# A decoder layer in one kernel: the cross-attention readout as three rounded products, standing between two groups of transposes

## The chip, the cores and the metric

The kernel runs on one core of a Trainium2 chip. The metric is the device time of one execution in microseconds (us). The core's engines work side by side, each through its own queue in order: PE (TensorE) multiplies matrices, and PEld is its loading of the stationary operand; DVE (VectorE) and ACT (ScalarE) do element work; POOL (GpSimd) does element work and issues indirect transfers; SP (SyncE) issues plain transfers. They wait for each other through semaphores, and a waiting instruction holds all that stands behind it on its engine.

## The reference

A pre-norm decoder layer for 32 batches of 128 tokens with 512 features, in float32. Three residual steps follow each other:

```
x = x + attention(layernorm(x))        # differential attention with rotary q and k
x = x + readout(layernorm(x), ctx)     # cross-attention on 128 context rows per batch
x = x + experts(layernorm(x))          # 48 experts, top 8 of each token
```

The step that the change touches is the second:

```
scores  = einsum('bsd,bmd->bsm', hidden, memory) * scale     # masked
attn    = softmax(scores)
readout = einsum('bsm,bmd->bsd', attn, memory)
```

`memory` is `ctx_2048`, one matrix of 128 rows by 512 per batch. The readout is one product of a 128x128 matrix of probabilities with that matrix.

## The kernel before

The first stage runs over the 32 batches in 38 turns. In each turn six batches stand at six different places of the layer: `norm` (batch t), `project` (t-1), `attend` (t-2), `cross` (t-3), `route` (t-4) and `slots` (t-5). The code calls them n, p, a, c, r and s. The first eight and the last turns are written out, the ones between are a hardware loop over pairs of turns. The second stage runs over the 48 experts and follows when all tokens are scattered into `slot_records`.

The order on each engine is written by hand: the function `turn` of each engine lists its instructions, and nothing reorders them. `x.after(b, "name")` in a wait is the semaphore count at which step `name` of batch b is done.

PE ends a turn with the transposes of q and of k (`transpose4`, L1170, into the PSUM banks `bank_tb` and `bank_ta`), then the readout (L1316). The next turn begins with the transposes of the normalized x, also into `bank_ta`; these wait until ACT has copied k out of that bank (`prj_a`, step `kT`). So the order around the bank is: probabilities transposed into `bank_ta` (L1300), copied by ACT to `xprobs_t`; k transposed into it, copied by ACT to `k_t`; x transposed into it. Then come the attention scores, which need `q_t` and `k_t`.

The readout is one float32 product of `xprobs_t` with `ctx_sb`; its records are two per batch. It writes `bank_r`, in which the router's counts stand too; it therefore waits until DVE has read these (`rte_v`, step `taken`, L1066). The projections are made otherwise (`product_r`, L1185): each operand is split into a high part, rounded to the type fp32r by an ACT copy, and a low part, the rest, made by a subtraction on DVE; three products high x high, high x low and low x high are summed in PSUM.

On DVE the end of a turn is: rotary sums (L1057, L1059), the counts `pos` and `taken` (L1064, L1066), `sq_mean` (L1070), a wait for POOL's `rstd_h` (L606), and `heads` (L1076), which PE transposes after the scores of the next turn.

On POOL a turn has eight indirect transfers (L544) and between them three powers for norms (L555: `rstd3` of the routed batch, `rstd1` of the new one, `rstd2` of the cross batch), a rotary sum (L598) and `rstd_h`. The transfer of row 0 waits for DVE's `token` (L850); `rstd2` is needed by DVE's `xn2` (L989), which PE transposes in the middle of the turn.

SP loads the context of the next cross batch in each turn, into one of two buffers; it waits until the readout of two batches ago is done.

## Time and profile before

| what | value |
|---|---|
| three runs | 1108.96, 1112.71 (median), 1113.69 us |
| profiled execution, first to last instruction | 1110.6 us |
| PE busy | 1032.1 us, 93% |
| DVE busy | 872.8 us, 79% |
| ACT busy | 628.9 us, 57% |
| POOL busy | 551.0 us, 50% |
| mean granted clock of PE | 0.981 |

The page gives the span of the profiled execution and no other time of it, so the span stands for its own time; the median of the runs is 2.1 us above it. Busy shares are means over both stages. The readout belongs to the first stage, which ends a little before 700 us. A row of a timeline gives start, length, engine, line of the kernel, output and input, and in brackets how long the engine had been idle before it and what ended that. Lengths of PE instructions overlap, since they are pipelined; the distance of two starts is what one costs in a row of them.

### The profile page before, as it was taken

How to read it: one execution, taken by the hardware profiler on the slowest of the kernel's cores; microseconds unless marked ns; L12 is line 12 of the kernel's file. 1: busy time of each engine (PE TensorE's matmuls, PEld its weight loads, DVE VectorE, ACT ScalarE, POOL GpSimd, SP SyncE). 2: the span in 40 equal slices, each digit the busy share in tenths (PEclk: the TensorE clock that was granted, in tenths of full speed). 3: DMA queues.
4: the chain of work that ended last, by engine and by line, in shares of the span. 5: the costliest groups of instructions: out<-in, count | busy, mean ns of one | idle time of the engine just before them, and what ended most of it. 6: DMA issues, size and time to landing. Idle time of an engine off the chain costs nothing.

```text
span 1110.6 us, 24896 instructions
## 1 busy us (share of the span) xinstructions
PE 1032.1 (93%) x6564; PEld 835.1 (75%) x6564; DVE 872.8 (79%) x2430; ACT 628.9 (57%) x1751; POOL 551.0 (50%) x529
## 2 busy tenths in 40 slices
PE   5999899999999999999999977999999999999892
PEld 4777777878878788787887856887777778778781
DVE  5777798888888798888888864677877778787771
ACT  4555445555554554555545441576767767676661
POOL 2124566666666666666666666333433334343333
PEclk9999899999999999999999998999999999999996
DMA  7999574543313122121221210599999999999983
GB/s 287 356 299 288 178 270 161 206 152 138 115 54 96 47 70 72 47 95 47 76 66 49 77 39 20 184 257 246 255 244 246 245 246 256 240 260 241 238 179 46
DMA packets 94051, 185.71 MB, mean 167 GB/s; under 512 B 24791, under 2 KB 24791, under 8 KB 93504
## 3 DMA queue, kind: packets, MB, share of 16 engines
q1 hardware_dynamic: 62640, 145.10, 40.2%
q0 software_dynamic: 31376, 40.20, 17.2%
q8 instruction: 16, 0.26, 0.1%
q14 instruction: 19, 0.16, 0.0%
HBM read 116.00 MB, written 122.00 MB: 214 GB/s over the span
## 4 chain that ended last, share of the span: by engine, by line
PE 26%; DMA 26%; issue 18%; POOL 13%; DVE 10%; ACT 3%; POOLq 1%; DVEq 1%; SPq 0%; ACTq 0%
DMA layer_out<-qk_both,scatter_idx 21%; PE ps L1185 13%; POOL slot_records L544 6%; PE ps L1170 5%; POOL layer_out L625 4%; DVE qk_both L1001 3%; POOL rstd L555 3%; PE ps L1175 2%; PE ps L1316 2%; DMA x_ln<-in_x 2%; PE ps L1212 1%; DVE diff L996 1%; PE ps L1283 1%; DMA slot_records<-row,slot_idx 1%; DMA w_raw<-slot_records 1%
## 5 line engine op out<-in xcount | busy, mean ns | idle before, releaser
L544 POOL DMA_INDIRECT slot_records<-row,slot_idx x256 | 266.1, 1040 | 88.5 <-issue 59.6
L625 POOL DMA_INDIRECT layer_out<-qk_both,scatter_idx x96 | 143.3, 1493 | 256.2 <-DVE scatter_idx L1102 205.3
L555 POOL TENSOR_TENSOR rstd<-mv,neg_half 128x1 f32<-128x1 f32 x96 | 80.0, 833 | 130.2 <-DVE mv L914 78.7
L1185 PE MATMUL ps<-w_high,xn_high 128*128 128x512 f32 x384 | 114.9, 422 | 0.7 <-ACT xn_high L640 0.7
L675 ACT ACTIVATE probs<-ps,neg_max_s 128x128 f32<-128x128 f32 x256 | 90.1, 378 | 33.6 <-DVE neg_max_s L911 33.6
L1341 PE MATMUL ps<-w_high 128*128 128x192 f32 x576 | 90.6, 279 | 19.6 <-DVE w_low L1088 19.2
L1185 PE MATMUL ps<-w_low,xn_high 128*128 128x512 f32 x384 | 108.6, 405 | 0.0
L1185 PE MATMUL ps<-w_high,xn_low 128*128 128x512 f32 x384 | 106.9, 400 | 0.0
L1341 PEld LDWEIGHTS ps<-w_high 128*128 128x128 f32 x576 | 76.0, 191 | 40.0 <-issue 39.3
L640 ACT ACTIVATE xn_t<-ps 128x512 f32<-128x512 f32 x64 | 38.3, 599 | 117.7 <-PE ps L1170 117.7
L1088 DVE TENSOR_TENSOR w_low<-gu_sb,w_high 128x1536 fp32r<-128x1536 f32 x48 | 84.3, 1757 | 7.4 <-ACT w_high L640 4.9
L1341 PE MATMUL ps<-w_high,w_low 128*128 128x192 f32 x576 | 87.8, 274 | 0.0
L1341 PE MATMUL ps<-w_low,w_high 128*128 128x192 f32 x576 | 87.7, 274 | 0.0
L1375 PE MATMUL ps<-w_high 128*128 128x512 f32 x192 | 81.2, 423 | 2.8 <-DVE w_high L1088 2.8
L1185 PEld LDWEIGHTS ps<-w_low,xn_high 128*128 128x128 f32 x384 | 71.4, 192 | 14.6
L1185 PEld LDWEIGHTS ps<-w_high,xn_low 128*128 128x128 f32 x384 | 70.4, 190 | 13.9
L1375 PE MATMUL ps<-w_high,w_low 128*128 128x512 f32 x192 | 75.9, 395 | 0.0
L1341 PEld LDWEIGHTS ps<-w_low,w_high 128*128 128x128 f32 x576 | 75.9, 192 | 0.0
L1341 PEld LDWEIGHTS ps<-w_high,w_low 128*128 128x128 f32 x576 | 75.9, 192 | 0.0
L1001 DVE TENSOR_TENSOR qk_both<-ps,rope_tab 128x1024 f32<-128x1024 f32 x64 | 75.1, 1215 | 0.7 <-PE ps L1185 0.7
L1185 PEld LDWEIGHTS ps<-w_high,xn_high 128*128 128x128 f32 x384 | 66.9, 193 | 10.7 <-ACT xn_high L640 1.1
L640 ACT ACTIVATE w_high<-h 128x192 fp32r<-128x192 f32 x144 | 51.7, 363 | 40.0 <-DVE h L1110 37.7
(165 smaller groups left out, 2462.0 us busy)
## 6 DMA issues: line engine op xcount, KB each, us to landing
gu_sb<-in_gate_up SPq DMA_DIRECT2D x48, 768.0 KB, 5.5
slot_records<-dn_both SPq DMA_DIRECT2D x6, 3366.0 KB, 22.9
w_raw<-slot_records SPq DMA_DIRECT2D x48, 280.5 KB, 4.7
dn_both<-in_down_proj SPq DMA_DIRECT2D x48, 256.0 KB, 3.2
x_ln<-in_x SPq DMA_DIRECT2D x32, 256.0 KB, 2.8
x_res<-in_x SPq DMA_DIRECT2D x32, 256.0 KB, 3.1
ctx_t_sb<-in_ctx_t SPq DMA_DIRECT2D x32, 256.0 KB, 3.6
ctx_sb<-in_ctx_rows SPq DMA_DIRECT2D x32, 256.0 KB, 4.2
```

Of the source, the lines that this page charges most:

```text
L544: pool.indirect_dma_start(out=records, out_offset=bass.IndirectOffsetOnAxis(ap=slot_idx[:, s.parity, k:k + 1], axis=0), in_=row[:, s.parit ...
L555: pool.tensor_tensor(rstd[:, :], mv[:, 1:2], neg_half[:, 0:1], ALU.pow).then_inc(steps.sem, 1)
L625: pool.indirect_dma_start(out=out, out_offset=bass.IndirectOffsetOnAxis(ap=scatter_idx[0:PART[h], d.parity, h:h + 1], axis=0), in_=y[0:PAR ...
L640: act.activation(dst, src, ACT.Copy).then_inc(steps.sem, 1)
L675: last = act.activation(probs[:, s, h, :], blocks(banks_s[:, s, :])[:, h, :], ACT.Exp, bias=neg_max_s[:, s, h:h + 1], scale=INV_SCALING, a ...
L1001: dve.tensor_tensor(buf[:, :, :, :].rearrange("p g r f -> p (g r) f"), qk, rope_tab[:, i:i + 1, :].to_broadcast([P, 4 * NH2, NF]), ALU.mul ...
L1088: return dve.tensor_tensor(dst, src, high.bitcast(FP32), ALU.subtract)
L1170: last = pe.transpose(blocks(bank)[:, c, :], src(c), ident[:, :])
L1175: last = pe.matmul(dst, left(c), right(c), start=(c == 0), stop=(c == n - 1))
L1185: last = pe.matmul(dst, left[:, c, :], right[:, m, c, :], start=(n == 0 and c == 0), stop=(n == 2 and c == KC - 1))
L1341: last = pe.matmul(dst, left[:, u.parity, k, cols], right[:, u.parity, k, :], start=(n == 0 and k == 0), stop=(n == 2 and k == KC - 1))
L1375: last = pe.matmul(dst, left[0:n, d.parity, 0, part(h)], right[0:n, d.parity, 0, :], start=(i == 0), stop=(i == len(pairs) - 1))
```

## The change

The readout is computed as the projections are: from a high and a low part of the probabilities and a high and a low part of the context. ACT now copies the transposed probabilities to `xprobs_high` where it copied them to `xprobs_t`, and gets one more copy per turn, `ctx_high`, between `heads_high` and the exponentials of the scores. POOL gets one subtraction per turn, `ctx_low`, behind `rstd3`. DVE gets one subtraction per turn, `xprobs_low`, behind the rotary sums. PE makes three products in place of one, and they stand between the transposes of q and the transposes of k; these now wait for `xprobs_low`, since it reads `bank_ta`. SP's wait for the readout becomes two waits, for the scores and for `ctx_low`.

```diff
@@ sync: turn
                     if c.back(2).exists():
-                        sp.wait_ge(crs_t.sem, crs_t.after(c.back(2), "readout"))
+                        sp.wait_ge(crs_t.sem, crs_t.after(c.back(2), "scores"))
+                        sp.wait_ge(ctx_p.sem, ctx_p.after(c.back(2), "low"))
@@ gpsimd: turn
+                def context_low():
+                    if c.exists():
+                        pool.wait_ge(ctx_a.sem, ctx_a.after(c, "high"))
+                        if c.back(1).exists():
+                            pool.wait_ge(crs_t.sem, crs_t.after(c.back(1), "readout"))
+                        pool.tensor_tensor(ctx_low[:, :], ctx_sb[:, c.parity, :], ctx_high[:, :].bitcast(FP32),
+                                           ALU.subtract).then_inc(ctx_p.sem, 1)
...
                 scale(out_p, out_v, o, rstd3, mv3)
+                context_low()
                 if early:
                     scatter_ready()
@@ scalar: turn
                     copy(heads_high[:, :, :], heads_t[:, :, :], hds_a)
+                if c.exists():
+                    act.wait_ge(d_ctx[c.parity], moved(c, 2))
+                    if c.back(1).exists():
+                        act.wait_ge(crs_t.sem, crs_t.after(c.back(1), "readout"))
+                    copy(ctx_high[:, :], ctx_sb[:, c.parity, :], ctx_a)
...
                     act.wait_ge(crs_t.sem, crs_t.after(c, "probsT"))
-                    copy(xprobs_t[:, :], bank_ta[:, 0:P], crs_a)
+                    copy(xprobs_high[:, :], bank_ta[:, 0:P], crs_a)
@@ vector: turn
+                if c.exists():
+                    dve.wait_ge(crs_a.sem, crs_a.after(c, "probsT"))
+                    if c.back(1).exists():
+                        dve.wait_ge(crs_t.sem, crs_t.after(c.back(1), "readout"))
+                    dve.tensor_tensor(xprobs_low[:, :], bank_ta[:, 0:P], xprobs_high[:, :].bitcast(FP32),
+                                      ALU.subtract).then_inc(crs_l.sem, 1)
                 if r.exists():
 
                     dve.wait_ge(rte_t.sem, rte_t.after(r, "counts"))
@@ tensor: turn
                     transpose4(bank_tb, lambda k: rot[:, k * P:(k + 1) * P]).then_inc(prj_t.sem, 1)
+                if c.exists():
+                    pe.wait_ge(crs_a.sem, crs_a.after(c, "probsT"))
+                    pe.wait_ge(ctx_p.sem, ctx_p.after(c, "low"))
+                    if r.exists():
+                        pe.wait_ge(rte_v.sem, rte_v.after(r, "taken"))
+                    pe.matmul(bank_r, xprobs_high[:, :], ctx_high[:, :], start=True, stop=False)
+                    pe.matmul(bank_r, xprobs_high[:, :], ctx_low[:, :], start=False, stop=False)
+                    pe.wait_ge(crs_l.sem, crs_l.after(c, "low"))
+                    pe.matmul(bank_r, xprobs_low[:, :], ctx_high[:, :], start=False, stop=True)\
+                        .then_inc(crs_t.sem, 1)
+                if p.exists():
                     pe.wait_ge(rope.sem, rope.after(p, "imag_k"))
                     if c.exists():
-                        pe.wait_ge(crs_a.sem, crs_a.after(c, "probsT"))
+                        pe.wait_ge(crs_l.sem, crs_l.after(c, "low"))
                     transpose4(bank_ta, lambda k: rot[:, DM + k * P:DM + (k + 1) * P]).then_inc(prj_t.sem, 1)
-                if c.exists():
-                    pe.wait_ge(crs_a.sem, crs_a.after(c, "probsT"))
-                    if r.exists():
-                        pe.wait_ge(rte_v.sem, rte_v.after(r, "taken"))
-                    pe.matmul(bank_r, xprobs_t[:, :], ctx_sb[:, c.parity, :], start=True, stop=True)\
-                        .then_inc(crs_t.sem, 1)
```

PE, end of a turn and start of the next, before (the eight transposes of `qk_rot` are four of q and four of k):

```order
L1170 MATMUL ps<-ident,qk_rot 128x128 x8
L1316 MATMUL ps<-ctx_sb,xprobs_t 128x512
L1170 MATMUL ps<-ident,xn 128x128 x4
L1212 MATMUL ps<-k_t,q_t 128x128 x8
L1170 MATMUL ps<-ident,heads 128x128 x4
```

The same place of the changed kernel (its line numbers are some 28 higher):

```order
L1198 MATMUL ps<-ident,qk_rot 128x128 x4
L1341 MATMUL ps<-ctx_high,xprobs_high 128x512
L1342 MATMUL ps<-ctx_low,xprobs_high 128x512
L1344 MATMUL ps<-ctx_high,xprobs_low 128x512
L1198 MATMUL ps<-ident,qk_rot 128x128 x4
L1198 MATMUL ps<-ident,xn 128x128 x4
L1240 MATMUL ps<-k_t,q_t 128x128 x8
```

The readout has moved in front of the four transposes of k, and nothing stands any more between these and the transposes of x, which use the same bank.

DVE, end of a turn in the changed kernel:

```order
L1079 TENSOR_TENSOR qk_rot<-qk_both 128x16x32
L1081 TENSOR_TENSOR qk_rot<-qk_both 128x8x32
L1087 TENSOR_TENSOR xprobs_low<-ps,xprobs_high 128x128
L1092 TENSOR_TENSOR pos<-ps,taken 128x48
L1094 TENSOR_TENSOR taken<-ps,taken 128x48
L1098 TENSOR_SCALAR sq_mean<-sq_sum 128x4
L1104 TENSOR_TENSOR heads<-ps,rstd_h 128x512
```

Before, the same rows stood there without `xprobs_low`; `pos`, `taken`, `sq_mean` and `heads` are now behind it.

POOL, first half of a turn in the changed kernel:

```order
L562 TENSOR_TENSOR rstd<-mv,neg_half 128x1
L573 TENSOR_TENSOR ctx_low<-ctx_sb,ctx_high 128x512
L551 DMA slot_records<-row,slot_idx 9216x561
L562 TENSOR_TENSOR rstd<-mv,neg_half 128x1
L551 DMA slot_records<-row,slot_idx 9216x561
L562 TENSOR_TENSOR rstd<-mv,neg_half 128x1
L551 DMA slot_records<-row,slot_idx 9216x561 x2
```

Before, the same rows without `ctx_low`; two transfers and the powers `rstd1` and `rstd2` are now behind it.

## Rows read from the trace of the kernel before

**Rows 1.** Busy us by stage: span, PE, PEld, DVE, ACT, POOL, granted clock, DMA share, GB/s.
```profile
300.00:500.00 200.00, 197.72 (x1215) 157.56 (x1214) 174.35 (x562) 107.61 (x380) 127.22 (x131) 1.00 0.22 67
```

**Rows 2.** Timeline of PE: readouts of batch 3 and of batch 29; start, length.
```profile
127.42 1.02 PE L1316 MATMUL ps<-ctx_sb,xprobs_t 128*128 128x512 f32 x2
...
642.87 1.02 PE L1316 MATMUL ps<-ctx_sb,xprobs_t 128*128 128x512 f32 x2
```

**Rows 3.** Timeline of all engines, end of one steady turn, start of the next.
```profile
304.62 1.19 PE L1170 MATMUL ps<-ident,qk_rot 128*128 128x128 f32 x8
...
304.82 0.28 ACT L640 ACTIVATE xprobs_t<-ps 128x128 f32<-128x128 f32 x1
304.91 0.21 DVE L1066 TENSOR_TENSOR taken<-ps,taken 128x48 f32<-128x48 f32 x1
...
305.04 0.16 DVE L1070 TENSOR_SCALAR sq_mean<-sq_sum 128x4 f32<-128x4 f32 x1
305.15 0.42 PEld L1170 LDWEIGHTS ps<-ident,qk_rot 128*128 128x128 f32 x4 [0.17 <-ACT xprobs_t L640]
...
305.64 1.02 PE L1316 MATMUL ps<-ctx_sb,xprobs_t 128*128 128x512 f32 x2
305.95 0.62 ACT L640 ACTIVATE k_t<-ps 128x512 f32<-128x512 f32 x1
306.36 0.69 DVE L1076 TENSOR_TENSOR heads<-ps,rstd_h 128x512 f32<-128x512 f32 x1 [1.17 <-POOL rstd_h L606]
...
306.61 0.42 PEld L1170 LDWEIGHTS ps<-ident,xn 128*128 128x128 f32 x4 [0.78 <-ACT k_t L640]
306.62 0.66 PE L1170 MATMUL ps<-ident,xn 128*128 128x128 f32 x4
...
307.46 0.60 ACT L640 ACTIVATE xn_high<-ps 128x512 fp32r<-128x512 f32 x1 [0.68 <-PE ps L1170]
```

**Rows 4.** The same timeline: DVE and POOL element operations in the turn before.
```profile
301.57 0.28 DVE L1024 TENSOR_TENSOR xscore_kept<-ps,mask_sb 128x128 f32<-128x128 f32 x1
301.71 0.73 POOL L598 TENSOR_TENSOR qk_rot<-qk_both 128x256 f32<-128x256 f32 x1 [1.60 <-DVE qk_both L1001]
...
301.98 0.61 DVE L1032 TENSOR_TENSOR xscore<-xscore_kept,mask_bias 128x128 f32<-128x128 f32 x1
```

**Rows 5.** The same timeline: PE, lengths of rounded products and of four transposes.
```profile
308.29 0.66 PE L1170 MATMUL ps<-ident,heads 128*128 128x128 f32 x4
...
309.71 1.10 PE L1185 MATMUL ps<-w_low,xn_high 128*128 128x512 f32 x4
...
310.65 1.09 PE L1185 MATMUL ps<-w_high,heads_high 128*128 128x512 f32 x4
```

**Rows 6.** The same timeline, middle of the turn: ACT, POOL, DVE and PE.
```profile
309.79 0.63 ACT L640 ACTIVATE heads_high<-heads_t 128x512 fp32r<-128x512 f32 x1
...
311.43 0.37 ACT L675 ACTIVATE probs<-ps,neg_max_s 128x128 f32<-128x128 f32 x1 [1.01 <-DVE neg_max_s L911]
...
311.49 1.07 POOL L555 TENSOR_TENSOR rstd<-mv,neg_half 128x1 f32<-128x1 f32 x1 [2.66 <-DVE mv L914]
...
313.57 1.03 POOL L544 DMA_INDIRECT slot_records<-row,slot_idx  x1 [1.01 <-DVE row L850]
...
316.45 0.96 POOL L555 TENSOR_TENSOR rstd<-mv,neg_half 128x1 f32<-128x1 f32 x1
...
317.54 0.55 DVE L989 TENSOR_SCALAR xn<-x,mv,rstd 128x512 f32<-128x512 f32 x1 [0.42 <-POOL rstd L555]
...
318.27 0.49 PEld L1170 LDWEIGHTS ps<-ident,xn 128*128 128x128 f32 x4
```

**Rows 7.** Timeline of PE around 114 us.
```profile
113.89 1.12 PE L1170 MATMUL ps<-ident,row 128*128 128x128 f32 x4 [4.81 <-DVE row L931]
```

**Rows 8.** Busy time by stage, columns as in Rows 1.
```profile
110.00:120.00 10.00, 6.12 (x19) 5.03 (x20) 5.73 (x19) 1.41 (x2) 3.16 (x4) 0.66 0.55 198
```

**Rows 9.** Timeline around 41 us, before any readout existed.
```profile
41.11 0.63 PE L1170 MATMUL ps<-ident,xn 128*128 128x128 f32 x4 [0.99 <-ACT k_t L640]
```

More of the change, by code:

```diff
@@ L182, in decoder_layer @@
         xsum = sb("xsum", [P, 1])
-        xprobs_t = sb("xprobs_t", [M, P])
+        xprobs_high = sb("xprobs_high", [M, P], FP32R)
+        xprobs_low = sb("xprobs_low", [M, P], FP32R)
+        ctx_high = sb("ctx_high", [M, DM], FP32R)
+        ctx_low = sb("ctx_low", [M, DM], FP32R)
         xinv = sb("xinv", [P, 1])
@@ L302, in decoder_layer @@
         crs_a = Steps(sem("cross_scalar"), "xT exp probsT")
+        ctx_a = Steps(sem("context_scalar"), "high")
+        ctx_p = Steps(sem("context_pool"), "low")
+        crs_l = Steps(sem("cross_vector_low"), "low")
         out_v = Steps(sem("readout_vector"), "inv coef x2 stats aggr eps normed")
@@ L576, in turn @@
                 scale(out_p, out_v, o, rstd3, mv3)
+                context_low()
                 if early:
```

## The prediction, made before the changed kernel ran

> **What bounds the kernel now.** I read the busy time by stage first. From 300 to 500 us PE is busy 197.7 of 200 us, at the full granted clock, DVE 174.4, POOL 127.2 and ACT 107.6 [rows 1]. So in the first stage PE sets the pace, and the reader should see how little it idles: 2.3 us in about ten turns, 0.23 us a turn. The readouts of batch 3 and batch 29 start at 127.42 and 642.87 us [rows 2]: 26 turns in 515.5 us, 19.8 us each. All that makes PE wait longer in a turn is paid once per turn, if no later wait of PE takes it up.
>
> Then I read the timeline at the turn's end, where the change works [rows 3]. PE issues the eight transposes of q and k from 304.62, and those of k wait for ACT's copy of the probabilities, which ends at 304.82 + 0.28 = 305.10. The readout starts at 305.64. The next transposes (of x) start at 306.61, and what they waited for is not the readout but ACT's copy of k, which ends at 305.95 + 0.62 = 306.57. So the readout, 0.98 us from its start to the next one's, lies beside ACT's copies of q and k; PE would have been free only about 0.1 us earlier. The readout costs nearly nothing today, and it is the cover for the copy of k.
>
> **The change, part by part.** I work out when the transposes of x can start in the changed kernel, on the clock of the same turn.
>
> 1. The copy to `xprobs_high` stands where `xprobs_t` stood and is taken as long: it ends at 305.10.
> 2. DVE is idle there and starts `xprobs_low` at about 305.15 (k's copy ends at 306.57 and PE follows at 306.61, so a semaphore is worth 0.04). The nearest row is the 128x128 product of PSUM with SBUF, 0.28 us [rows 4]. Behind it stand `pos` and `taken`, 0.21 each [rows 3], which in the trace were done beside the copy at 305.12. Now 305.15 + 0.28 + 0.21 + 0.21 = 305.85.
> 3. PE's readout waits for `taken`. The transposes of q are out by 305.15, so PE idles 0.70 us until 305.85. The wait for `xprobs_low` in front of the third product is met by then. `ctx_low` is made ten microseconds earlier and holds nothing.
> 4. Three rounded products: four of them take 310.65 - 309.71 = 0.94 us [rows 5], so three take 0.70 and end the issue at 306.55. (The float32 readout took 0.98 with the wait.)
> 5. Four transposes of k, 0.66 us from the first start to the last end [rows 5]: 307.21. ACT's copy follows its transposes by 0.18 (306.62 + 0.66 = 307.28 against 307.46 for `xn_high`) [rows 3]: 307.39 to 308.01. The transposes of x start at 308.05.
>
> Against 306.61 that is 1.44 us later, in each turn. Of it 0.70 is the wait for `taken`, and 0.74 is the uncovered way from the transposes of k over ACT to the transposes of x, less what the shorter products give.
>
> What else moves. `sq_mean` starts at 305.04 in the trace and will start near 305.8, so `heads` comes 0.7 to 0.8 later than 306.36 [rows 3]. Its transposes on PE start at 308.29 today and at 309.7 then, while `heads` ends near 307.8: hidden. The copy `ctx_high` (0.63, as `heads_high`) falls into the idle time of 1.01 us that ACT has in front of the exponentials [rows 6]; with 0.63 of 1.01 used nothing is late. If it were not hidden, it would delay the exponentials only, which have slack to the third projection. SP's two waits are for steps of a batch two back, done long before, and its queue issues as before.
>
> POOL's subtraction is the term with no row of its own. The nearest is the 128x256 sum of two SBUF operands, 0.73 us [rows 4]: twice the elements, 1.46, is what I take. Below it is bounded by 0.73. Above: it may have to share with DVE. `xscore`, the one 128x128 operation with two SBUF operands beside POOL's sum, takes 0.61 where `xscore_kept` takes 0.28, and it ends just after POOL's (301.98 + 0.61 against 301.71 + 0.73) [rows 4]. With DVE's `heads_low` of about 0.7 in its way POOL's would be 2.15.
>
> The Trainium skill, GPSIMD Engine Reference, section 1 (Specifications), says that GpSimd's SBUF interfaces are shared with VectorE and contend with DVE instructions that have two SBUF inputs; the row of `xscore`, 0.61 us, agrees. Its section 3.1 gives 4497 ns for a two-input operation of 2048 elements; an estimate by that page would be a quarter, 1.12 us, and the sum below would stay as it is. No run here shows that size yet.
>
> Where it stands: POOL ends `rstd3` at 311.49 + 1.07 = 312.56 and idles 1.01 until the first transfer at 313.57. 1.46 us there push the transfer, `rstd1`, the second transfer and `rstd2` by 0.45 to 0.50 against DVE's chain. DVE's chain itself is then about 0.95 later, since its `xn_low` awaits ACT's copy of x (307.46 + 1.44 + 0.60 = 309.50). Together 1.45. PE at that place is 1.44 later, and has 0.18 of slack (`xn2` ends at 317.54 + 0.55 = 318.09, its transposes load at 318.27) [rows 6]. So POOL's subtraction costs nothing on top, as long as it is under some 1.6 us: its cover is the very delay at the turn's end. Were that delay not there, it would cost some 0.3 to 0.5 itself.
>
> **The sum.** Batches 3 to 29 pay in full: 27 x 1.44 = 38.9 us. The turns of batches 1 and 2 would pay 2.9, and batch 0, behind whose transposes of k five small products of the router's gate stand, about 0.5; but PE then idles 4.81 us at 113.89, behind a DVE row that waits for scattered records [rows 7]. If these transfers end when they did, that idle time takes up all of it. I count half, 1.7. Batches 30 and 31 have no transposes of k; they pay the 0.70 of DVE's three operations each, 1.4. Together 42.0 us. The second stage is untouched and starts later by the same. 1110.6 + 42.0 = 1152.6 for the profiled execution; on the median of 1112.7, 1154.7, so 1155 us.
>
> **Bounds.** Per turn at least 0.74 (if the wait for `taken` is covered after all): 27 x 0.74 = 20, so 1133. At most 1.44 + 0.55 (POOL's subtraction at 2.15, 0.55 over the 1.6 that is covered) = 2.0: 54 + 4.8 = 59, so 1172.
>
> **Rivals.**
> - The bubble in front of the products is not there: DVE's three operations overlap more than their lengths say, or PE's issue runs late anyway. For it: starts on DVE lie closer than lengths (`taken` at 304.91, `sq_mean` at 305.04). Against: `taken` needs `pos`, and `pos` needs nothing but stands behind `xprobs_low`. Then 1133 to 1143, with 1136 as its middle.
> - POOL becomes the bound: the subtraction takes 2 us or more, `xn2` is late, and PE waits a second time in the middle of the turn. For it: the shared access in rows 4. Against: DVE works little with two SBUF operands from 313 to 315. Time 1166 to 1175.
> - PE's clock falls. After the idle 4.81 us at 113.89 four transposes take 1.12 us, not 0.6 [rows 7], and the granted clock from 110 to 120 us is 0.66, a mixture of the 1.2 and the 2.4 GHz level [rows 8]. Two new idle times of 0.7 and 0.9 us inside 2.5 us, once a turn, could do the same. Against: 0.99 us idle at 41.11 [rows 9] is followed by transposes of the usual 0.63 us. If 5 us of each turn ran at half speed, that is 2.5 us more a turn, 27 x 3.9 = 106, so 1219. The Trainium skill, TensorE: Matmul & The Clock Gate, section "A second HAM failure mode: psum-queue depth-cycling", says that short idles between groups of matmuls can make the clock swing between its levels. That speaks against this change; the row at 41 us does not bear it out.
> - Not slower. The place would be a later wait of PE in the same turn that takes up the delay, because another engine sets the pace there; then only the shorter products count, (0.98 - 0.70) x 27 = 7.6 us, so 1105. It decides from 1.44 us of such waiting a turn. The profile has 0.23 [rows 1]. It is the weakest of the rivals, unless the delay itself is wrongly worked out, which needs the copy of k to end as early as now, though its transposes are issued behind three products more.
>
> **How the numbers follow.** The forecast as worked out (1143 to 1166) 0.62; no bubble 0.17; POOL 0.13; clock 0.02; not slower, or within the measurement, 0.06. The likeliest gives 1155. The range, 1134 to 1171, takes the forecast whole and most of both neighbours. About 0.5%, 5.5 us, is what a measurement of this kernel tells from no change: faster 0.03, same 0.03, slower 0.94.
>
> **What would show it.** In the profile of the changed kernel: turns of about 21.3 us; an idle time of PE of about 0.7 us in front of the first of the three products, ended by DVE `taken`; one of about 0.9 us in front of the transposes of x, ended by ACT `k_t`; POOL's subtraction near 1.5 us; no new wait in front of the transposes of `xn2`; the granted clock as before. The forecast is wrong if the transposes of x follow those of k by less than 0.9 us, if PE waits for POOL in mid-turn, or if the second stage has changed its length.

## The result

| | median | lowest to highest | runs |
|---|---|---|---|
| before | 1113.2 us | 1108.96 to 1114.89 | 4 |
| after | 1170.68 us | 1166.13 to 1172.78 | 4 |

The changed kernel takes 1.0513 times as long, 95% interval 1.0481 to 1.0545: 57.5 us more. 1155 was forecast, with a range from 1134 to 1171. The direction is right, and the time lies at the very edge of the range: 42 us more had been worked out.

### The profile page after: what moved, and what is told of

The parts are those of the page before. It is cut to its first block, busy times and chain, and to the rows that moved or that the text cites. A ratio compares the mean times of both kernels' runs of the same rounds, so it can differ in the third digit from the quotient of the medians.

```text
span 1169.5 us, 25235 instructions
## 1 busy us (share of the span) xinstructions
PE 1037.2 (89%) x6596; PEld 849.3 (73%) x6596; DVE 906.1 (77%) x2462; ACT 647.2 (55%) x1783; POOL 589.8 (50%) x561
## 4 chain that ended last, share of the span: by engine, by line
issue 30%; DMA 24%; POOL 21%; DVE 10%; PE 9%; ACT 3%; POOLq 2%; SPq 1%; DVEq 0%; ACTq 0%
DMA layer_out<-qk_both,scatter_idx 19%; POOL slot_records L551 12%; DVE qk_both L1023 5%; POOL rstd L562 4%; POOL layer_out L642 3%; DMA ctx_sb<-in_ctx_rows 3%; PE ps L1213 2%; DVE diff L1018 2%; PE ps L1198 2%; PE ps L1374 1%; POOL qk_rot L615 1%; POOL rstd_h L623 1%; DMA gu_sb<-in_weights 1%; PE ps L1408 1%; DMA w_raw<-slot_records 1%
## 5 line engine op out<-in xcount | busy, mean ns | idle before, releaser
L1198 PE MATMUL ps<-ident,xn 128*128 128x128 f32 x256 | 42.9, 292 | 43.2 <-ACT k_t L657 22.4
```

The lines of the kernel that those rows point to most:

```text
L1198: last = pe.transpose(blocks(bank)[:, c, :], src(c), ident[:, :])
```

## The profile after

Busy time of the same stretch as in [rows 1]; columns as there:

```profile
300.00:500.00 200.00, 181.83 (x1094) 148.09 (x1093) 165.89 (x513) 102.30 (x351) 124.45 (x126) 0.97 0.20 64
```

PE idles 18.2 of 200 us where it idled 2.3, and every other engine is less busy too: no other engine became the bound, and the work is strung out. The granted clock is 0.97, no longer 1.00.

The readouts of batch 3 and batch 29 (in [rows 2] at 127.42 and 642.87) start at 131.49 and 700.97. That is 569.5 us for 26 turns, 54.0 more than before. The 4.1 before batch 3, 1.8 in the turn of batch 29, 0.1 in that of batch 30 and -1.1 in all that follows make up the rest of 58.9, the difference of the two spans (1169.5 and 1110.6).

The end of one steady turn, all engines, in the order of start (start, length, engine, line, output and input, idle time before and its end). It answers to [rows 3]:

```profile
303.16 0.31 PE L1328 MATMUL ps<-ident,xprobs 128*128 128x128 f32 x1
303.31 0.60 PE L1198 MATMUL ps<-ident,qk_rot 128*128 128x128 f32 x4
...
303.81 0.29 ACT L657 ACTIVATE xprobs_high<-ps 128x128 fp32r<-128x128 f32 x1
...
304.14 0.29 DVE L1087 TENSOR_TENSOR xprobs_low<-ps,xprobs_high 128x128 fp32r<-128x128 f32 x1 [0.75 <-ACT xprobs_high L657]
304.34 0.20 DVE L1092 TENSOR_TENSOR pos<-ps,taken 128x48 f32<-128x48 f32 x1
...
304.58 0.21 DVE L1094 TENSOR_TENSOR taken<-ps,taken 128x48 f32<-128x48 f32 x1
...
304.93 0.47 PE L1341 MATMUL ps<-ctx_high,xprobs_high 128*128 128x512 f32 x1 [1.02 <-DVE taken L1094]
...
305.71 0.60 PE L1198 MATMUL ps<-ident,qk_rot 128*128 128x128 f32 x4
...
306.35 0.60 ACT L657 ACTIVATE k_t<-ps 128x512 f32<-128x512 f32 x1 [1.27 <-PE ps L1198]
...
307.09 0.63 PE L1198 MATMUL ps<-ident,xn 128*128 128x128 f32 x4 [0.78 <-ACT k_t L657]
```

Both forecast idle times of PE are there, ended by `taken` and by `k_t`. The second is 0.78 us (0.69 in every other turn). The first is 1.02 instead of 0.70. ACT ends `xprobs_high` at 304.10 and the transposes of x start 2.99 later; the prediction had 305.10 and 308.05, 2.95. So that chain is right to 0.04. (Inside it two errors cancel: the three products take 0.78 from the first start to the next transpose and not 0.70, the way over k 1.38 and not 1.50.) What is not right is its start: the transpose of the probabilities starts at 303.16 and ACT's copy 0.65 behind it. Before, the copy stood at 304.82 [rows 3], 0.35 behind this transpose:

```profile
304.47 0.31 PE L1300 MATMUL ps<-ident,xprobs 128*128 128x128 f32 x1
```

The reason lies ten microseconds further on in the turn, where POOL makes `ctx_low`:

```profile
310.69 0.61 ACT L657 ACTIVATE ctx_high<-ctx_sb 128x512 fp32r<-128x512 f32 x1
...
311.53 0.37 ACT L697 ACTIVATE probs<-ps,neg_max_s 128x128 f32<-128x128 f32 x1 [0.23 <-DVE neg_max_s L933]
...
311.59 1.06 POOL L562 TENSOR_TENSOR rstd<-mv,neg_half 128x1 f32<-128x1 f32 x1 [3.09 <-DVE mv L936]
...
312.64 1.27 POOL L573 TENSOR_TENSOR ctx_low<-ctx_sb,ctx_high 128x512 fp32r<-128x512 f32 x1
312.69 1.51 DVE L953 TENSOR_SCALAR row<-x,mv,rstd 128x512 f32<-128x512 f32 x1
...
315.42 0.57 POOL L562 TENSOR_TENSOR rstd<-mv,neg_half 128x1 f32<-128x1 f32 x1 [0.30 <-DVE mv L967]
...
317.40 0.98 POOL L562 TENSOR_TENSOR rstd<-mv,neg_half 128x1 f32<-128x1 f32 x1 [0.20 <-DVE mv L997]
...
318.50 0.55 DVE L1011 TENSOR_SCALAR xn<-x,mv,rstd 128x512 f32<-128x512 f32 x1 [0.42 <-POOL rstd L562]
...
319.10 0.42 PEld L1198 LDWEIGHTS ps<-ident,xn 128*128 128x128 f32 x4 [0.23 <-DVE xn L1011]
```

`ctx_high` fits into ACT's idle time, as forecast: of the 1.01 in [rows 6] 0.23 is left. `ctx_low` takes 1.27, less than the 1.46 that were counted. But DVE's `row`, which starts 0.05 after it, takes 1.51. The groups of DVE by line over 300 to 500 us (busy time, mean ns of one, idle before) show that it is no exception; first the kernel before, then the changed one:

```profile
L931 DVE TENSOR_SCALAR row<-x,mv,rstd 128x512 f32<-128x512 f32 x10 | 5.5, 549 | 0.3
```

```profile
L953 DVE TENSOR_SCALAR row<-x,mv,rstd 128x512 f32<-128x512 f32 x9 | 11.5, 1277 | 0.3
...
L1011 DVE TENSOR_SCALAR xn<-x,mv,rstd 128x512 f32<-128x512 f32 x9 | 4.9, 546 | 5.9 <-POOL rstd L562 5.9
```

Seven of these nine take 1.42 to 1.52; in the other two (533 and 535 ns) `row` started behind `ctx_low`, and another instruction was caught, as the last section shows. The same operation on the same shape, `xn`, stays at 546 ns: no `ctx_low` runs beside it. POOL's rows above show the rest of the way: `rstd1` and `rstd2` waited for nothing but their place in the queue before, and here they wait for DVE's `mv`. So DVE's chain sets POOL's, and `xn2` arrives after PE is ready: its transposes load 0.23 us late. The prediction had said that no new wait would stand there, and that the clock would stay; both signs came out against it.

Where PE waited for other engines (total us, times, longest), after:

```profile
PE ps L1341 <- DVE taken L1094: 30.6, 31, 2.0
PE ps L1198 <- ACT k_t L657: 22.4, 30, 0.8
...
PE ps L1198 <- DVE xn L1011: 8.2, 14, 2.3
```

And four of the 26 turns from batch 3 to batch 29 (those of 12, 14, 15 and 27) ran partly at the lower clock; in the kernel before none did. The start of the turn behind the readout of batch 12:

```profile
328.71 0.97 PE L1198 MATMUL ps<-ident,xn 128*128 128x128 f32 x4 [0.69 <-ACT k_t L657]
```

Four transposes take 0.97 instead of 0.63. The eight short products of the scores behind them take 2.08 us from first start to the start of `heads`' transposes, where other turns take 1.16. The 20 us windows around it:

```profile
300.00:320.00 20.00, 18.09 (x112) 14.69 (x111) 16.84 (x56) 10.93 (x39) 13.04 (x14) 1.00 0.27 97
320.00:340.00 20.00, 18.30 (x104) 14.68 (x104) 16.46 (x52) 10.74 (x39) 11.54 (x13) 0.91 0.26 78
```

0.91 is a mixture of the 1.2 and the 2.4 GHz level. It comes directly behind two idle times, 1.01 and 0.69 us, that the old kernel did not have. In the turn of batch 15 the clock fell behind another idle time, one of 2.28 us for `xn2` (1.53 in the kernel before):

```profile
409.85 0.66 PE L1198 MATMUL ps<-ident,xn 128*128 128x128 f32 x4 [2.28 <-DVE xn L1011]
...
413.33 1.05 PE L1198 MATMUL ps<-ident,diff 128*128 128x128 f32 x4
```

There four transposes take 1.05 and not 0.60. That idle time goes back to POOL, which stood still for 2.89 us in front of a transfer (2.72 in the kernel before), for no reason that the profile shows.

## Experiments

In the steady state a turn can be cut in two: from the transpose of the probabilities to the transposes of x (part A, where the change works), and from there to the next transpose of the probabilities (part B, the other 17.5 us). The two numbers of each field are two turns in a row, since the loop is over pairs. These are medians of differences of starts on PE between 250 and 500 us of each profile. Each ratio is against runs of the kernel before on the same chip; their medians were 1113.8 us for the first four experiments, 1115.04 for `ctx_low` later and the filled gap, and 1114.89 for the last row.

| kernel | part A | part B | turn | measured against before (95%) |
|---|---|---|---|---|
| before | 2.15, 2.37 | 17.50, 17.47 | 19.65, 19.84 | 1 |
| after | 3.92, 3.83 | 17.81, 17.96 | 21.73, 21.79 | 1.0513 (1.0481 to 1.0545) |
| order only | 3.01, 3.10 | 17.51, 17.46 | 20.52, 20.56 | 1.0179 (1.0137 to 1.0221) |
| parts only, old order | 2.82, 2.73 | 18.40, 18.57 | 21.22, 21.30 | 1.0370 (1.0337 to 1.0403) |
| `xprobs_low` behind the counts | 3.09, 3.18 | 17.95, 17.81 | 21.04, 20.99 | 1.0285 (1.0252 to 1.0318) |
| without `ctx_low` | 3.51, 3.59 | 17.50, 17.47 | 21.01, 21.06 | 1.0336 (1.0294 to 1.0378) |
| `ctx_low` later | 3.51, 3.61 | 17.49, 17.47 | 21.00, 21.08 | 1.0323 (1.0261 to 1.0384) |
| gap filled | 3.84, 3.91 | 17.97, 17.82 | 21.81, 21.73 | 1.0488 (1.0415 to 1.0561) |
| only the order left | 2.86, 2.94 | 17.50, 17.47 | 20.36, 20.41 | 1.0152 (1.0105 to 1.0198) |

In this table part B is 17.5 us wherever `ctx_low` does not stand beside `row`, and 17.8 to 18.6 wherever it does.

### The order alone

The kernel before, with its one float32 readout moved in front of the transposes of k.

```diff
                     transpose4(bank_tb, ...)        # q
+                if c.exists():
+                    pe.wait_ge(crs_a.sem, crs_a.after(c, "probsT"))
+                    if r.exists():
+                        pe.wait_ge(rte_v.sem, rte_v.after(r, "taken"))
+                    pe.matmul(bank_r, xprobs_t[:, :], ctx_sb[:, c.parity, :], start=True, stop=True)...
                     transpose4(bank_ta, ...)        # k
-                if c.exists(): ...                  # the same readout
```

> The kernel before with the change's order alone: the single float32 readout stands between the transposes of q and of k; no high and low parts, no subtraction on POOL or DVE. A steady turn takes about 19.75 us before and 21.75 us in the changed kernel. Theory (two costs: the order uncovers k's copy, and the parts add waits of their own): PE starts the readout right behind the transposes of q (about 0.5 us earlier than before), needs 0.85 us for it, then the transposes of k, ACT's copy (0.6 us), the transposes of x: about 0.9 us more per turn, 20.65 us, and a time near 1139 us; no wait for xn2 in mid-turn. Rival (the order is the whole cost, and the parts are hidden): 21.5 us or more per turn, 1165 us or more.

Measured 1135.3 us (1130.05 to 1137.65), 21.5 more than before, and turns of 20.5 us, near the 20.65 of the theory. The longest of the new waits of PE:

```profile
PE ps L1170 <- ACT k_t L640: 22.5, 30, 0.8
```

That is the same wait, of the same length, as in the changed kernel; one for `taken` is not there. So the uncovered copy of k is shown, and priced: 0.8 us a turn with the float32 readout.

### The parts alone

The changed kernel with the transposes of k back in front of the products.

```diff
+                if p.exists():
+                    pe.wait_ge(crs_l.sem, crs_l.after(c, "low"))
+                    transpose4(bank_ta, ...).then_inc(prj_t.sem, 1)     # k
                 if c.exists():
                     ...                                                 # three products
-                if p.exists(): ...                                      # the same transposes
```

> The changed kernel with its three products back at the old place, behind the transposes of k (these still wait for xprobs_low, since it reads the same bank). Theory: the products are covered by ACT's copies again; what stays is 0.3 us at the transposes of k, which now wait for DVE's subtraction and not only for ACT's copy, and 0.3 to 0.5 us in mid-turn, where POOL's subtraction makes xn2 late: turns of 20.4 to 20.6 us, about 1132 to 1137 us. Rival (the order is nothing, the added work is all): above 1160 us. With the order theory alone and no cost of the parts: 1113 us.

Measured 1156.06 us (1152.99 to 1159.7): the expectation is missed by some 20 us. It had counted 0.3 to 0.5 us in mid-turn, for POOL's own length. The timeline of DVE and POOL, and PE in front of the transposes of `xn2`:

```profile
309.42 1.28 POOL L573 TENSOR_TENSOR ctx_low<-ctx_sb,ctx_high 128x512 fp32r<-128x512 f32 x1
309.47 1.52 DVE L953 TENSOR_SCALAR row<-x,mv,rstd 128x512 f32<-128x512 f32 x1
...
315.89 0.66 PE L1198 MATMUL ps<-ident,xn 128*128 128x128 f32 x4 [0.51 <-DVE xn L1011]
```

POOL's length is what it was in the changed kernel, and it is `row` that grows beside it. Part B is 1.0 us longer than before, although PE has the old order. (The other 0.5 is in part A: the transposes of k wait 0.67 us for `xprobs_low`.)

### `xprobs_low` behind the counts

```diff
                 if r.exists():
                     ...                             # pos, taken
+                if c.exists():
+                    dve.tensor_tensor(xprobs_low[:, :], bank_ta[:, 0:P], ...)
                 if a.exists():                      # sq_mean
```

with the same four lines taken away in front of `pos`.

> The changed kernel with DVE's xprobs_low behind the counts (pos, taken) and not in front of them. Theory: PE's first two products no longer wait for taken, and the third waits for xprobs_low, which is ready some 0.35 us after the copy. The idle time of 1.0 us in front of the products goes down to that of ACT's copy, 0.3 to 0.5 us; 0.5 to 0.7 us less per turn at the end of the turn, of which 0.2 to 0.3 us may come back in mid-turn, where less delay covers POOL. Turns of 21.1 to 21.4 us, 1152 to 1160 us. Rival (the wait for taken only looks like a cost, since ACT or the third product's operand is as late): unchanged, 1168 us or more.

Measured 1144.51 us (1141.62 to 1147.56). The turn is 0.74 us shorter than the changed kernel's, and the wait for `taken` is gone; what is left of it there is

```profile
313.60 0.50 PE L1341 MATMUL ps<-ctx_high,xprobs_high 128*128 128x512 f32 x1 [0.24 <-ACT xprobs_high L657]
```

Turn and time came out below what was expected: 0.24 us of the wait are left where 0.3 to 0.5 were expected, and the 0.2 to 0.3 that were to come back in mid-turn did not come. Part B keeps its extra 0.4 us.

### Without `ctx_low`

POOL's subtraction is left out and the second product reads `ctx_high` again, so the low part of the context is missing from the readout.

```diff
-                context_low()
...
-                    pe.matmul(bank_r, xprobs_high[:, :], ctx_low[:, :], start=False, stop=False)
+                    pe.matmul(bank_r, xprobs_high[:, :], ctx_high[:, :], start=False, stop=False)
```

> The changed kernel without POOL's subtraction: the second product reads ctx_high in place of ctx_low, so the low part of the context is left out of the result. PE makes as many products. Theory (what went beyond the forecast is POOL's subtraction, which holds DVE's row in mid-turn at 1.51 us where it took 0.55): row takes 0.55 us again, PE waits for xn2 no more, DVE and ACT are 0.3 us earlier at the turn's end, and the idle time in front of the products falls from 1.0 to 0.7 us: turns of 21.2 us, about 1155 us. Rival (it is PE's own issue or the three operations on DVE being slower than reckoned): row short again, but the turn stays at 21.7 us, 1168 us or more.

Measured 1149.08 us (1148.42 to 1155.45), a turn of 21.0 us, a little below the theory and far from the rival. `row` is as before the change, and the wait for `taken` is what the prediction had:

```profile
L951 DVE TENSOR_SCALAR row<-x,mv,rstd 128x512 f32<-128x512 f32 x10 | 5.5, 548 | 0.3
```

```profile
315.10 0.28 ACT L655 ACTIVATE xprobs_high<-ps 128x128 fp32r<-128x128 f32 x1
...
316.20 0.47 PE L1339 MATMUL ps<-ctx_high,xprobs_high 128*128 128x512 f32 x1 [0.70 <-DVE taken L1092]
```

### `ctx_low` later

The whole computation, with `ctx_low` moved on POOL from behind `rstd3` to in front of the rotary sum, where DVE multiplies operands out of PSUM.

```diff
                 scale(out_p, out_v, o, rstd3, mv3)
-                context_low()
...
+                context_low()
                 if p.exists():
                     pool.wait_ge(rope.sem, rope.after(p, "sin"))
```

> The changed kernel with POOL's subtraction ctx_low moved from behind rstd3 to the place in front of POOL's rotary sum, where POOL idles 1.6 us and DVE works on operands in PSUM. All work is done. Theory (the cost in mid-turn is the place of the subtraction, beside DVE's row, and not its length on POOL): row takes 0.55 us again, no wait for xn2, the turn as without the subtraction, 21.0 us, and 1148 to 1153 us. Rival (POOL has no room for 1.28 us more in a turn anywhere): the rotary sum or rstd_h is late, 21.5 us or more, 1162 us or more.

Measured 1150.33 us (1150.07 to 1153.46), as the theory had it. Part A and part B are those of the kernel without the subtraction, to 0.02 us. The timeline around it:

```profile
303.96 0.55 DVE L953 TENSOR_SCALAR row<-x,mv,rstd 128x512 f32<-128x512 f32 x1
...
310.33 2.35 DVE L1023 TENSOR_TENSOR qk_both<-ps,rope_tab 128x1024 f32<-128x1024 f32 x2
311.27 1.29 POOL L573 TENSOR_TENSOR ctx_low<-ctx_sb,ctx_high 128x512 fp32r<-128x512 f32 x1
```

POOL's subtraction takes the same 1.29 us and costs nothing: the two rotary products beside it, whose one large operand is in PSUM, take 1216 ns each on average over the stretch, as before the change. So it is not POOL's time that costs 0.72 us a turn (21.76 - 21.04, means of two turns), but the DVE instruction that it stands beside.

### The second gap half filled

One product of 256 columns whose result nobody reads, between the transposes of k and those of x.

```diff
                     transpose4(bank_ta, ...).then_inc(prj_t.sem, 1)     # k
+                    if c.exists():
+                        keep_busy(1)
```

> The changed kernel with one product of 256 columns that nobody reads (0.4 us) on PE between the transposes of k and those of x, where PE idles 0.7 to 0.8 us. In four steady turns of the changed kernel's profile the scores take 2.08 us and not 1.16 (the lower clock level), and the turn is 0.83 us longer. Theory of the clock (the two idle times so close together let it fall now and then): no turn with scores of 2.08 us, some 3 us less in all, 1165 to 1169 us. Rival (the falls come by something else): such turns again, same time. In neither case does the turn at full clock, 21.7 us, change.

Measured 1166.44 us (1164.86 to 1177.9). PE's idle time in front of the transposes of x falls to 0.34 (0.25 in every other turn):

```profile
303.01 0.63 PE L1198 MATMUL ps<-ident,xn 128*128 128x128 f32 x4 [0.34 <-ACT k_t L657]
```

The turns are as long as the changed kernel's other ones, and no turn between batches 3 and 29 runs at the lower clock, against four there. (The expectation speaks of four turns with scores of 2.08 us; the trace has three, and the fourth fall is that of batch 15.) It speaks for idle time as the trigger, but not more. With both gaps and `ctx_low` later one turn fell, without `ctx_low` none. The wait of 2.28 us in the turn of batch 15 is here too, and this time no fall follows it: that turn takes 23.86 us from readout to readout, 25.07 in the changed kernel. Each is one trace, and the times of this kernel and the changed one can't be told apart.

### Only the order left

PE's order as changed, with both of the edits already shown at once:

```diff
-                context_low()                       # POOL, behind rstd3
+                context_low()                       # in front of the rotary sum
...
-                    dve.tensor_tensor(xprobs_low[:, :], bank_ta[:, 0:P], ...)   # DVE, in front of pos
+                    dve.tensor_tensor(xprobs_low[:, :], bank_ta[:, 0:P], ...)   # behind taken
```

> The changed kernel with two edits at once: xprobs_low behind the counts on DVE, and ctx_low in front of the rotary sum on POOL. The order on PE stays the changed one. If the costs add up as I read them, only the uncovered copy of k is left: PE waits 0.7 to 0.8 us for k_t in each turn, for nothing else, row takes 0.55 us, turns are 20.4 to 20.6 us as with the order alone, and the time is 1.016 to 1.021 of the kernel before. The rival is that the longer chain on DVE and ACT (sq_mean behind xprobs_low, which gave 0.25 us a turn where all three costs had been taken off) adds to the order's cost: turns of 20.7 to 20.9 us, ratio 1.023 to 1.028. It would show as further waits of PE, of about 0.25 us, for xprobs_high or heads_low.

Measured 1132.76 us (1128.53 to 1134.93), a turn of 20.36 and 20.41, just below the theory and not near the rival. The costs nearly add: the two edits save 0.74 and 0.72 alone and 1.37 together, of 2.01. Its only wait in a steady turn:

```profile
313.34 0.65 PE L1198 MATMUL ps<-ident,xn 128*128 128x128 f32 x4 [0.69 <-ACT k_t L657]
```

The three products save 0.15 us a turn against the float32 readout at the same place (part A 2.90 against 3.05, means).

### All three costs off, and three steps further

Then I tried to keep the rounded products without their price. First: old order on PE, `xprobs_low` behind the counts, `ctx_low` later, and the probabilities transposed into a PSUM bank of their own, so that k's transposes need not wait for `xprobs_low`.

```diff
+        xprobs_ps = ps[:, 7, 0:P]
...
-                    pe.transpose(bank_ta[:, 0:P], xprobs[:, :], ident[:, :]).then_inc(crs_t.sem, 1)
+                    pe.transpose(xprobs_ps, xprobs[:, :], ident[:, :]).then_inc(crs_t.sem, 1)
```

> The three products with their high and low parts, but: behind the transposes of k (old place); the probabilities transposed into another PSUM bank, so that the transposes of k wait for no reader of them; xprobs_low behind the counts; ctx_low in POOL's idle time in front of the rotary sum. Theory (the whole cost of the change is these waits, and the added work itself is hidden): turns of 19.6 to 19.8 us as in the kernel before, 1105 to 1116 us, the transposes of x again waiting for ACT's copy of k. Rival (some of the added work costs by itself, on ACT with ctx_high or on DVE): 20.1 us or more per turn, 1123 us or more.

Measured 1121.77 us (1120.77 to 1127.24, 12 runs), ratio 1.0072 (1.0044 to 1.0100): nearly all is back, but not all. A turn is 20.0 us on average, 0.25 over the old one; that lies between the theory (19.8) and the rival (20.1), and neither came true. Two waits of PE are left in it, one for `k_t`, one in the loading of the operand for `heads_low`:

```profile
307.78 0.66 PE L1199 MATMUL ps<-ident,xn 128*128 128x128 f32 x4 [0.17 <-ACT k_t L658]
...
313.66 0.77 PEld L1214 LDWEIGHTS ps<-w_high,heads_low 128*128 128x128 f32 x4 [0.27 <-DVE heads_low L943]
```

Second: the same, with ACT's copy of v behind those of q and k.

```diff
-                    copy(v_sb[:, p.parity, :], bank_v, prj_a)
                     copy(q_t[:, :, :], blocks(bank_tb), prj_a)
                     copy(k_t[:, :, :], blocks(bank_ta), prj_a)
+                    copy(v_sb[:, p.parity, :], bank_v, prj_a)
```

> The kernel of the run before this one, with ACT's copy of v behind the copies of q and k. Theory (the copy of k ends the turn, and it starts as soon as its transposes are done, so v in front of it costs little): 0.05 to 0.25 us per turn less than that kernel, as the transposes of k are some 0.2 us earlier now: 1098 to 1112 us. Rival (the scores then wait for v): the same or longer than that kernel.

1121.92 us (1117.51 to 1136.14, 12 runs), ratio 1.0057 (1.0027 to 1.0088) without the longest run. The expectation is missed, the rival's time came true, but not by its wait. The wait for `k_t` is gone and the turn is the same, 19.90 and 20.08 from readout to readout: PE now waits for `heads_low` instead, and what part A loses (0.37) part B gains. Such a swap of one wait for another suggests that PE is no longer what sets the pace, but the chain over ACT's `xprobs_high`, DVE's `xprobs_low`, `sq_mean`, POOL's `rstd_h` and `heads`. That was argued from the trace, and the next two runs were to test it.

Third, therefore, `xprobs_low` behind `sq_mean`, with the old and with the new place of v; and the kernel before with only the bank of its own and v last, to see what these are worth without the rounded products.

```diff
-                    dve.tensor_tensor(xprobs_low[:, :], xprobs_ps, ...)
                     dve.tensor_scalar(sq_mean[:, :], sq_sum[:, :], ...)
+                    dve.tensor_tensor(xprobs_low[:, :], xprobs_ps, ...)
```

> The kernel e8_three_costs_off with xprobs_low one place later on DVE, behind sq_mean, where DVE waits 1.2 us for POOL's rstd_h anyway. In that kernel a turn still took 20.0 us against 19.75 before, and sq_mean started behind xprobs_low, which itself had waited 0.25 us for ACT's copy. Theory (the rest is that delay of sq_mean, rstd_h, heads and DVE's whole chain behind it): 0.2 to 0.3 us less per turn, 19.7 to 19.8 us, 1110 to 1116 us. Rival (the rest is ACT's ctx_high or PE): 20.0 us and 1120 us or more, as there.

> The same with ACT's copy of v behind those of q and k. In e9_and_v_last that took the wait for k_t away, but the turn did not shorten, and PE waited for heads_low instead. Theory (DVE's chain sets the pace there, and it is 0.3 us earlier now): 19.4 to 19.7 us per turn, 1101 to 1112 us, and faster than the kernel before by 0 to 1%. Rival (ACT or PE sets the pace then): as e10, 1110 to 1116 us.

> The kernel before with its single float32 readout, the probabilities transposed into another PSUM bank (the transposes of k wait for no copy) and v copied last. It tells what the three products are worth where their waits are gone. Theory (PE's own order limits this one: the float32 readout takes 0.85 us, the three products 0.70): 19.5 to 19.7 us per turn, 1105 to 1112 us, some 0.1 us a turn longer than e11. Rival (the products are worth nothing, DVE's chain limits both): the same as e11 or shorter.

These three ran on another chip. The kernel before took 1136.33 us (1130.01 to 1145.22, 29 runs) on it, so only ratios are read. In this order they are 1.0041 (1.0013 to 1.0069), 0.9983 (0.9952 to 1.0014) and 0.9982 (0.9952 to 1.0011). The first misses its expectation and stays a little slower than the kernel before: in its trace PE now waits for `xprobs_low` itself, 19 times for 7.7 us in all. So the chain that I had named is not shown as the cause. The second is the rounded readout with its price removed, the third the old readout with the same freedom: neither can be told from the kernel before, nor from each other, and the 0.1 us a turn that I expected between them is too small for these intervals. No version is shown to be faster than the kernel before. There is no trace of that kernel from this chip, so turns can't be compared. What set the pace of a turn in these last traces, where waits on `k_t`, `heads_high` and `xprobs_low` alternate, stays open.

## Why the prediction was right in its direction and short in its size

**The wait for `taken`: right.** 0.70 us was forecast and 0.70 stands where nothing else is disturbed. Taking it away saves 0.66 to 0.74 a turn.

**The uncovered way over ACT's copy of k: right, a little too large.** 0.74 forecast, 0.64 measured (part A 2.90 against 2.26). ACT's chain itself came within 0.04.

**POOL's `ctx_low` "costs nothing on top": this is the step that failed.** I had one question of it, how long POOL is occupied, took 1.46 us for it, and found a cover of 1.6 us in the delay at the turn's end. The length was even shorter, 1.28 us on average. But I did not ask which DVE instructions stand beside it. `row` takes 0.73 us longer on average. DVE's whole chain behind it is then late against PE: it costs 0.40 in part B, where `xn2` comes late, and 0.32 in part A, where ACT's copy of the probabilities starts 0.65 instead of 0.35 behind their transpose, and the wait for `taken` grows to 1.02. Together 0.72 a turn, about 19 us over 27 turns, on a term that the sum had at nothing. Two experiments remove exactly this, one by leaving the work out and one by moving it, and agree.

That the time still lies in the range is in part luck. Its upper end came from 0.55 us a turn for a subtraction of 2.15 us on POOL; that did not happen, and 0.72 came by the other way, less 0.14 that part A had been given too much.

**The rival "POOL becomes the bound"** had 0.13 and names the right place: PE waits a second time in mid-turn, near 1170 us. Its condition, 2 us or more on POOL, was not met; DVE was held instead. I had read the shared access in [rows 4], where `xscore` takes 0.61, and used it in one direction only, as what DVE could do to POOL. And I had the rule for operations with two inputs in mind, so `row`, which has one, was not looked at.

The Trainium skill had the other half of that rule. The GPSIMD Engine Reference, section 1 (Specifications), names as contending also DVE instructions in a 2-port perf mode, and VectorE: DVE Perf Modes, section "Mode 2×_2P — use both read ports for one tensor", says that a float32 `tensor_scalar` between SBUF operands can run in it. `row` is such an instruction, and the trace agrees: 549 ns alone, 1277 beside `ctx_low`. Which mode it ran in, no row shows.

**The clock** had 0.02, worked out as 5 us of every turn at half speed, 106 us. It fell in four turns of 26, and one such turn is 0.8 to 1.2 us longer. That is 3.8 us in this trace: the falls exist, but at a size for which the prediction had neither a term nor a rival.

**Early turns and tail.** 1.7 forecast for batches 0 to 2, 4.1 measured; 1.4 for the last two batches, 0.1 measured, and -1.1 behind them. Neither was tested apart. The turn of batch 15 is 3.3 us longer than before and not 2.0; 1.2 of that is the fall of the clock behind its wait for `xn`, as the same turn with the gap filled shows. The kernel before had its 1.53 us wait there too, which is most of the 2.3 us that PE idles in [rows 1]: in the other turns there was next to no slack.

In sum, for batches 3 to 29: 38.9 forecast; -3.8 (27 x 0.14, part A without POOL's effect 1.30, not 1.44), +19.4 (27 x 0.72), +3.8 (clock), +0.1 (the rest of batch 15) make 58.4; measured are 55.8 (54.0 and 1.8). Most of the other 2.6 are turns at both ends: batches 3, 26, 28 and 29 pay 1.0 to 1.9 us instead of 2.0.

**Not slower, and no bubble**: the first is refuted by the time, the second by the wait, which is longer than forecast.

## What to carry to other kernels

When work is given to an idle engine, its length there is half the question: list what runs beside it on the engine that shares its memory access, and move it beside work that reads PSUM. When a matrix product is moved, ask first what it has been covering; here one readout of 1 us hid a copy of 0.6 us and its two semaphores, and cost next to nothing where it stood; without that cover the turn was 0.8 us longer. And cost the chain that feeds an engine, not only the engine: with all three costs off, removing one wait of PE brought up another, and the turn stayed as long.

## What the runs showed of the hardware that I had not expected

A DVE `tensor_scalar` of 128x512 float32 with one large SBUF input takes 546 to 549 ns alone and 1.42 to 1.52 us when it starts just after a 1.28 us two-input subtraction on POOL. POOL's own length is the same beside it (1.27 to 1.28) and elsewhere (1.29).

That DVE is held and not slowed in proportion is seen in two ways. First, `row` ends 0.28 to 0.29 us behind POOL's subtraction in all 25 turns of the changed kernel in which it starts inside it, however late that is: in the steady turn above at 314.20 (POOL at 313.91), and here, started 0.72 us into it, at 140.57 (POOL at 140.28), after only 0.85 us. And where DVE was first, by 0.16 us, it was POOL that took longer. (First by only 0.08 us, in the kernel with the parts alone, `row` was held all the same and took 1.62 us.) The rows, both pairs from the changed kernel:

```profile
118.23 0.55 DVE L953 TENSOR_SCALAR row<-x,mv,rstd 128x512 f32<-128x512 f32 x1 [5.16 <-DMA slot_records<-row,slot_idx]
118.39 1.53 POOL L573 TENSOR_TENSOR ctx_low<-ctx_sb,ctx_high 128x512 fp32r<-128x512 f32 x1 [5.27 <-ACT ctx_high L657]
...
139.00 1.28 POOL L573 TENSOR_TENSOR ctx_low<-ctx_sb,ctx_high 128x512 fp32r<-128x512 f32 x1
139.72 0.85 DVE L953 TENSOR_SCALAR row<-x,mv,rstd 128x512 f32<-128x512 f32 x1 [0.75 <-DMA slot_records<-row,slot_idx]
```

Second, a turn where a much smaller instruction stood there (DVE and POOL, changed kernel; and its group in the kernel before):

```profile
334.76 1.29 POOL L573 TENSOR_TENSOR ctx_low<-ctx_sb,ctx_high 128x512 fp32r<-128x512 f32 x1 [0.68 <-ACT ctx_high L657]
335.06 1.01 DVE L869 TENSOR_SCALAR slot_idx<-slot 128x8 int32<-128x8 f32 x1 [0.15 <-DVE slot L864]
...
336.05 0.54 DVE L953 TENSOR_SCALAR row<-x,mv,rstd 128x512 f32<-128x512 f32 x1
```

```profile
L847 DVE TENSOR_SCALAR slot_idx<-slot 128x8 int32<-128x8 f32 x10 | 1.8, 180 | 0.9 <-DVE slot L842 0.8
```

Eight elements, 180 ns on average before, take 1.01 us and end at 336.07, with POOL's subtraction (336.05). So the price hardly depends on DVE's size. It is the rest of POOL's instruction less about 0.2 us: 0.83 of 0.99 here, 0.96 of 1.22 for `row` in the steady turn.

POOL's two-input operation on SBUF took 730 ns for 256 elements per partition and 1282 to 1295 ns for 512, so about 2.2 ns an element and 0.18 us fixed (worked out from the two). The Trainium skill, GPSIMD Engine Reference, section 3.1, gives 4497 ns for 2048; an estimate by this line would be 4.6 us. No run here has that size.

Behind idle times of 1.02 and 0.69 us, once in a turn of 21.7 us, the clock fell in three turns and stayed in the others; behind one of 2.28 us it fell in the changed kernel and stayed in the one with the filled gap.
